# A two-layer decoder kernel: longer ring of PSUM banks, moved copies and scatters, and a causal mask split between TensorE and GpSimd

## What is computed

```python
x = layernorm(x + attention16(layernorm_affine(x)))        # phase 0 (A), 16 heads of 64, 512 x 512 scores
x = layernorm(x + cross16(x, ctx))                         # phase 1 (B), 16 heads, 77 keys
x = layernorm(x + moe_top2(x))                             # phase 2 (C), 8 experts
x = layernorm(x + gated_attention(x))                      # phase 3 (D)
x = layernorm(x + cross8(x, ctx))                          # phase 4 (E), 8 heads, 77 keys
x = layernorm(x + moe_top1(x))                             # phase 5 (F)

def gated_attention(x):                                    # 16 heads of 64
    q, k, v = silu(x @ Wq), silu(x @ Wk), x @ Wv
    cum = cumsum(-softplus(x @ Wa + ba))                   # per head, over the 512 positions
    decay = exp(where(causal, cum[i] - cum[j], -inf))
    o = (q k^T * decay) @ v
    o = groupnorm(o) * gn_w + gn_b                         # per head
    return (o * sigmoid(x @ Wg)) @ Wo
```

## Time and profile before

| | |
|---|---|
| median of 3 runs (lowest, highest) | 1533.67 us (1532.97, 1536.28) |
| the profiled execution's own time | 1532.61 us |
| its span in the trace | 1530.8 us |
| mean granted TensorE clock | 0.927 of full speed |
| PE busy in the span | 83% |
| DVE, ACT, POOL busy in the span | 52%, 55%, 35% |

### The profile page before, as it was taken

The page is one execution under the profiler, slowest core; times in us unless marked ns, Lnnn a source line. Parts: engine busy times, 40 slices in busy tenths (PEclk is TensorE's granted clock), DMA queues, the critical chain, the costliest instruction groups (busy, mean ns, idle before and its releaser), DMA issues. The chain is left out here.

```text
span 1530.8 us, 22554 instructions
## 1 busy us (share of the span) xinstructions
PE 1276.4 (83%) x6934; PEld 735.2 (48%) x6934; DVE 801.0 (52%) x2448; ACT 839.1 (55%) x1902; POOL 530.0 (35%) x606
## 2 busy tenths in 40 slices
PE   5999999999999988877861994899999996786452
PEld 2334443444344335545431993576676764454251
DVE  3543454354334435366653235878675766567425
ACT  4777677767767753554430563567575653453121
POOL 2554455545545531212243351132223222112332
PEclk9999999999999999999885997999999997997686
DMA  8335343330000000000013671100000000000053
GB/s 211 57 62 83 63 71 60 57 80 1 1 1 1 1 1 0 1 1 0 3 58 131 195 208 48 42 1 1 1 1 1 1 1 28 0 1 8 23 153 100
DMA packets 77556, 67.29 MB, mean 44 GB/s; under 512 B 5024, under 2 KB 68640, under 8 KB 77184
## 3 DMA queue, kind: packets, MB, share of 16 engines
q1 hardware_dynamic: 73488, 57.69, 16.6%
q0 software_dynamic: 3520, 7.27, 1.3%
q10 hardware_dynamic: 432, 0.89, 0.2%
HBM read 37.42 MB, written 28.41 MB: 43 GB/s over the span
## 5 line engine op out<-in xcount | busy, mean ns | idle before, releaser
L1960 POOL TENSOR_TENSOR work<-work 128x512 f32<-128x512 f32 x256 | 266.1, 1039 | 271.6 <-DVE work L1438 271.6
L1013 ACT ACTIVATE work<-bank,work 128x512 f32<-128x512 f32 x256 | 176.5, 689 | 116.7 <-DVE work L1430 116.7
L1430 DVE TENSOR_REDUCE work<-bank 128x1 f32<-128x512 f32 x256 | 176.6, 690 | 77.5 <-PE bank L547 77.5
L555 PEld LDWEIGHTS bank<-cst,work 128*128 128x128 f32 x1024 | 110.4, 141 | 163.8 <-issue 103.5
L555 PE MATMUL bank<-cst,work 128*128 128x128 f32 x1024 | 159.7, 283 | 6.3 <-ACT work L1021 6.1
L1438 DVE RECIPROCAL work<-work 128x1 f32<-128x1 f32 x256 | 41.9, 164 | 223.4 <-ACT work L1013 223.1
L1021 ACT ACTIVATE work<-bank 128x512 f32<-128x512 f32 x256 | 152.6, 596 | 0.5 <-PE bank L555 0.5
L547 PE MATMUL bank<-work 64*128 64x512 f32 x512 | 144.5, 641 | 3.4 <-ACT work L1013 3.4
L2000 POOL TENSOR_TENSOR work<-work 128x1232 f32<-128x1232 f32 (+1 forms) x32 | 55.5, 1734 | 254.9 <-DVE work L1512 254.8
L565 PE MATMUL bank<-work 128*64 128x512 f32 x512 | 137.4, 617 | 0.7 <-ACT work L1021 0.7
L494 PE MATMUL bank<-OT,W 128*128 128x512 f32 x208 | 95.7, 604 | 1.2 <-DVE am L1618 0.7
(11 more groups left out here) (258 smaller groups left out, 2443.6 us busy)
## 6 DMA issues: line engine op xcount, KB each, us to landing
xs<-gat SPq DMA_DIRECT2D x18, 1040.0 KB, 13.1
W<-in_w SPq DMA_DIRECT2D x30, 322.0 KB
W<-in_w SPq DMA_DIRECT2D x23, 193.0 KB
work<-xs SPq DMA_DIRECT2D x62, 65.0 KB
gat<-yt SPq DMA_DIRECT2D x12, 256.0 KB, 3.4
work<-in_w SPq DMA_DIRECT2D x9, 322.0 KB
W<-in_v SPq DMA_DIRECT2D x1, 2048.0 KB, 12.3
x_ext<-in_x SPq DMA_DIRECT2D x4, 256.0 KB, 7.5
```

The costliest lines, as they stand in the source:

```text
L555: m = nc.tensor.transpose(out[:, k * P:(k + 1) * P], pA[u % 5][:, k * P:(k + 1) * P], ident)
L1013: A(pA[u % 5], bank[u % 3][:, :], ACT.Exp, bias=nmax[:, u % 8:u % 8 + 1], accum_out=rsum[0][:, u % 8:u % 8 + 1]).then_inc(sem("a_e"), 1)
L1430: V.tensor_reduce(nmax[:, u % 8:u % 8 + 1], bank[u % 3][:, :], AX, ALU.max, negate=True)\
L1960: G.tensor_tensor(pA[u % 5], pA[u % 5], rsum[1][:, u % 8:u % 8 + 1].to_broadcast([P, S]), ALU.mult)\
```

## The change

1. The ring of `take_next` is a list that PE sets anew: banks 5, 6, 7 in phase B, banks 2, 5, 6, 7 in phase E, 5, 6, 7 for the tiles of both moe phases, and 6, 7 again in phase D (and A).
2. On ACT, in a step with t = 1 of a cross phase, the copies of the outputs come ahead of the step's exp.
3. POOL scatters batch 0 at the start of the moe phase, after its part of the last tail, and no longer at u = 15 of the cross loop.
4. In phase D the mask matmul (L821, two a group) is gone. Partitions 96 to 127 of the stationary and the moving operand of L819, unused before, now carry a coarse mask: it puts 1e30 where the row index lies beyond the diagonal's group of 4. POOL fills the groups' masks once at the start of D.
5. What is left above the diagonal, inside each group of 4, POOL zeroes after ACT's exp, with one `affine_select` of 128x512 f32 in place per head (`mask_fine`, two a group); DVE's `d_at` waits for it.
6. `d_decays` is one matmul with a 128-wide stationary operand in place of two with 64. The operands of L811 and L819 were broadcast columns; now POOL writes them out with three copies of 96x128 bf16 a group (`pick`), two groups ahead.
7. DVE's wait for POOL's preparation (`d_zero`) moves from the start of D to just before `d_lsel`; PE waits for `d_zero`, or for the product `d_qe` of two groups before, ahead of `d_decays`. The mask and identity tiles that DVE built at the start of the program are gone.

```diff
         turn = [0]
+        ring = [6, 7]
         def take_next(pe, key, reader, value):
-            i = 6 + turn[0] % 2
+            i = ring[turn[0] % len(ring)]
...
+                ring[:] = [5, 6, 7] if ph == 1 else [2, 5, 6, 7]
                 cross_q(c, 0)
                 cross_kv(c)
...
+                ring[:] = [5, 6, 7]
                 loaded(pe, "w" + m_["n"], DMA_COUNT["w" + m_["n"]])
...
             def d_decays(g):
-                for hh in range(2):
-                    m = mm(out[hh * DH:(hh + 1) * DH, :], sel[:, 2 * p + hh:2 * p + hh + 1].to_broadcast([P, DH]),
-                           lsel_b[b % 2], start=True, stop=True)
-                m.then_inc(sem("d_lp"), 1)
+                if g < 2:
+                    pe.wait_ge(sem("d_zero"), 1)
+                else:
+                    pe.wait_ge(sem("d_qe"), g - 1)
+                out = take(pe, 0, sem("d_el"), g + 1)
+                mm(out[:, :], selE[g % 2][:, :], lsel_b[b % 2], start=True, stop=True).then_inc(sem("d_lp"), 1)
             def d_decay_to(g, hh):
-                mm(out[:, :], sel[:, 2 * p + hh:2 * p + hh + 1].to_broadcast([P, P]), lsel_b[b % 2],
-                   start=True, stop=False)
-                mm(out[:, :], ident_b[:, :], mask[:, :], start=False, stop=True).then_inc(sem("d_la"), 1)
+                mm(out[:, :], selM[2 * (g % 2) + hh][:, :], lsel_b[g // 8 % 2], start=True, stop=True).then_inc(sem("d_la"), 1)
...
+                    if t == 1 and b >= 1:
+                        cross_o(c, b - 1)
                     if b < NB:
                         cross_exp(c, b, t)
-                    if t == 1 and b >= 1:
-                        cross_o(c, b - 1)
...
             def d_at(g):
-                    dve.wait_ge(sem("d_dm"), 2 * g + hh + 1)
+                    dve.wait_ge(sem("d_mk"), 2 * g + hh + 1)
...
                     cross_tail(tail, c["w0"], u)
-                    if u == 15:
-                        moe_scatter(MOE[ph + 1], 0)
...
                 tail(m_["w0"] - 1, 0)
+                moe_scatter(m_, 0)
                 moe_scatter(m_, 1)
...
-                G.memset(lselD, 0.0).then_inc(sem("d_zero"), 1)
+                group = lselD.bitcast(BF16)[3 * 32:P, :]
+                link(G.memset(lselD[0:3 * 32, :], 0.0))
+                link(G.memset(group, 1.0))
+                zero = pool.to_reg(0.0)
+                link(G.affine_select(group, group, [[0, 2 * NT], [1, P]], ALU.is_ge, zero, base=0, channel_multiplier=-4))
+                link(G.affine_select(group, group, [[0, 2 * NT], [-1, P]], ALU.is_ge, zero, base=3, channel_multiplier=4))
+                for i in range(2):
+                    link(G.memset(selE[i][3 * 32:P, :], 0.0))
+                for i in range(4):
+                    link(G.memset(selM[i][3 * 32:P, :], 1e30))
+                    link(G.affine_select(selM[i][3 * 32:P, :], selM[i][3 * 32:P, :], [[1, P]], ALU.is_ge, zero, base=-4,
+                                         channel_multiplier=-4))
+                def pick(g):
+                    for hh in range(2):
+                        h = 2 * (g % 8) + hh
+                        G.tensor_copy(selM[2 * (g % 2) + hh][0:3 * 32, :], sel[0:3 * 32, h:h + 1].to_broadcast([3 * 32, P]))
+                    p = 2 * (g % 8)
+                    return G.tensor_copy(selE[g % 2][0:3 * 32, :].rearrange("k (h d) -> k h d", h=2),
+                                  sel[0:3 * 32, p:p + 2].unsqueeze(2).to_broadcast([3 * 32, 2, DH]))
+                def mask_fine(g, hh):
+                    pool.wait_ge(sem("d_dm"), 2 * g + hh + 1)
+                    dm = v3(dmD[g % 2][:, hh * S:(hh + 1) * S], NT)
+                    G.affine_select(dm, dm, [[0, NT], [1, P]], ALU.is_ge, zero, base=0, channel_multiplier=-1)\
+                        .then_inc(sem("d_mk"), 1)
+                pick(0)
+                pick(1).then_inc(sem("d_zero"), 1)
...
+                mask_fine(0, 0)
+                mask_fine(0, 1)
                 for g in range(32 + 5):
                     b, s = g // 8, g % 8
+                    if g + 2 < 32:
+                        pool.wait_ge(sem("d_dm"), 2 * g + 2)
+                        pick(g + 2)
                     if g < 32:
...
                         G.tensor_tensor(qeD[g % 3], qTD[g % 2], elD[g % 3], ALU.mult).then_inc(sem("d_qe"), 1)
+                    if g + 1 < 32:
+                        mask_fine(g + 1, 0)
+                        mask_fine(g + 1, 1)
```

More of the change, by code:

```diff
@@ L109, in decoder @@
         cst = sb("cst", [P, NKEPT])
-        mask = sb("mask", [P, S], BF16)
-        ident_b = sb("ident_b", [P, P], BF16)
+        selM = [sb(f"selM{i}", [P, P], BF16) for i in range(4)]
+        selE = [sb(f"selE{i}", [P, P], BF16) for i in range(2)]
         sel = sb("sel", [P, H], BF16)
@@ L885, in phase_d @@
             def phase_d():
+                ring[:] = [6, 7]
                 loaded(pe, "D", DMA_COUNT["D"])
@@ L1444, in _ @@
             V.tensor_scalar(x_ext[:, :, D + 1], const("slot")[:, 0:NB * NT], 2.0, None, ALU.mult)
-            V.tensor_copy(ident_b[:, :], ident)
-            V.tensor_copy(sel[:, :], const("sel"))
-            for t in range(NT):
-                i = V.tensor_scalar(mask[:, t * P:(t + 1) * P], after, 1e30, None, ALU.mult)
-            i.then_inc(consts_ready, 1)
+            V.tensor_copy(sel[:, :], const("sel")).then_inc(consts_ready, 1)
             NU = NB * UNITS
@@ L1876, in phase_d @@
                 enter(dve, 3)
-                dve.wait_ge(sem("d_zero"), 1)
                 loaded(dve, "D", DMA_COUNT["D"])
@@ L1884, in phase_d @@
                 d_split_w(2)
+                dve.wait_ge(sem("d_zero"), 1)
                 d_lsel(0)
```

1 line of the change is left out of this document (removed).

## The result

The changed kernel takes 1515.53 us (median of 4 runs, 1513.62 to 1517.65) against 1533.89 us (4 runs): a ratio of 0.9878, 95% interval 0.986 to 0.9896. It is faster by 18.4 us where 50 were forecast. The profiled execution has a span of 1514.4 us, against 1530.8 before.

A forecast was written before the change was run, and what follows sets the result against it. The prediction took D to be bound by PE and B and E to be held by waits for banks, copies and POOL's scatters. It summed 28 (B) + 14 (E) + 8 (D) = 50 us, forecasting 1484, range 1461 to 1516.

The forecast's parts named there:

- PE leaves after the fifth copy, about 5.0 instead of 7.6: Outputs in B: with three banks PE finishes a batch at ACT's copying pace, 2.6 us sooner.
- opening 5: Opening of B: the first 24 us of q, k and v products get 5 us shorter in all.
- the loop's q: q products in B's loop: three times 1.7 us, 5 us, limited by when ACT finishes.
- E's 8: Outputs in E: four pairs written without waiting; three batches give 1.6 + 3.4 + 3.5 = 8 us.
- counted 28: Phase B: terms sum to 33 us, 28 counted because PE then meets DVE's subtraction sooner.
- counted 14: Phase E: terms sum to 21.5 us, only 14 counted because engines wait for each other in turn.
- counted 8: Phase D: half of PE's 17.7 us saving, 9, less 1 for the first uncovered select.
- I keep half, 9: Phase D: of PE's 17.7 us saving 9 stays, since DVE must follow and POOL's added reads hold it.
- (a): Rival: GpSimd's reads hold DVE in D, so the 9 us become -12, giving 1504; chance 0.22.
- (b): Rival: waits removed in B and E return elsewhere, only half kept, 21 + 8 = 29, giving 1504; chance 0.13.
- (c): Rival: all is kept, 33 + 21.5 + 17.7 = 72 us, giving 1461; chance 0.10.
- (d): Rival: slower, a dear select (4.5 us) makes POOL set D's pace, giving 1567; chance 0.05.

The follow-up runs named there:

- part_D: The kernel before with only the change of phase D (the changed kernel with parts 1 to 3 undone): 1537.19 us, ratio 1.0022.
- part_D_late: The kernel before with only the change of phase D, POOL's three copies placed behind the selects: 1528.98 us, ratio 0.9974.
- parts123: The kernel before with the ring, the order of output copies and the scatter changed, phase D untouched: 1513.52 us, ratio 0.9863.
- late_gate_last: The changed kernel with POOL's copies behind the selects and, on PE, k's transposes and the output products ahead of the gate projection: 1515.02 us, ratio 0.9887.
- late_two_copies: The changed kernel with copies behind the selects, two a group, and the two 64-row decay matmuls with broadcast columns back: 1506.13 us, ratio 0.9823.

## Why the prediction was wrong, point by point

**Where the number failed.** Two steps failed, the larger one outside D. "PE leaves after the fifth copy, about 5.0 instead of 7.6" took ACT's copies for the pace and gave PE no price of its own. Eight products of 512 f32 columns take PE 7.03 us without any bank to wait for. This price stood in the kernel before, in L494's row. So q's eight went from 7.70 to 7.13, v's stayed, eight pairs of outputs stop at 7.09, and four pairs in E at 3.65 where 2.6 was forecast. The terms "opening 5", "2.6" and "4" of the outputs, the loop's q and E's 8 lose most of what they held. What stayed is what had been a wait: the exp ahead of the copies (13.7 to 7.1, forecast 5.4, measured 6.6) and part of the end of B.

The same sum has no term for PE's clock in B. The batch at 729, given 4 us, went from 10.29 to 9.42 at a granted 0.75; the last one, given 2.6, went from 7.60 to 8.70 at 0.81. Both follow a wait of over 4 us for ACT, which the change leaves in place.

**B** counted 28. The twelve profiles with the three parts reach the first scores of D at 939.6 to 947.8 us, on average 943.6; the three without any of them (before, part_D, part_D_late) at 954.8 to 958.4, on average 956.5. That is 13. **E** counted 14: its stretch behind D's last scores is 8.7 and 8.5 us shorter in the two profiles of the changed kernel. **All outside D** counted 42, measured 20.3 and, in the second set, 21.0.

**End of B.** The wait for L1618 is gone and L1997 no longer stands behind the scatters, both as said. The outputs begin at 769.20. That is 780.28 - 769.20 = 11.1 us earlier, where 5 + 12 + 5 + 8.8 = 30.8 were to have come forward by then. The cover named for the scatter, POOL's 14.79 us of idle, held: the eight scatters end at 776.04 and the next start at 781.90.

**D** counted 8: measured 1.0 and 0.8 in the two profiles, nothing in the two comparisons by medians (parts123 is as fast), and 3.4 us lost alone, though not in D's length. The saving on PE was about rightly priced: 17.7 forecast, PE busy some 19 to 20.8 us less, and 13.1 us of time when POOL adds nothing. The step that failed is "I keep half, 9", with "behind a waiting POOL stand only pick, d_qe and the group norm's chains, which have about a step". The copies stand ahead of qe and the selects, and where POOL comes late from the chain there is no step to spare. With the copies behind them D is 301.1 and 302.9 us, 8.1 and 6.3 under before. So my 8 is about the value of the change with another order of its own instructions, as long as the three parts outside D are there; alone it is worth 5.8 us of D and 3.5 of the time. The 5.0 us between 301.1 and 296.1 are about what POOL's added work costs D even in the better order.

**The rivals.** (a) named the mechanism, "the second select, the copies and d_qe now stand back to back", and its sign in D against my 8, but with 21 us of damage (9 to -12) where all that POOL gained cost 12.1 (D 296.1 to 308.2), 7.1 of it by order alone; its total of 1504 missed too, as it kept my 42. The Trainium skill (SBUF — State Buffer, Who interferes with whom), cited there, fits the rows: L1823 (two SBUF inputs) is held until the product ends, L1809 (one in PSUM) stays at 0.683. (b), half kept outside D, had the number of its half: 21 forecast, 20.3 measured; with D at 0 it would have given 1513. Its reason holds only in part, so the number was partly luck: in B PE's waits for ACT's L1124 did grow, from 7.8 to 12.7 us, but those for DVE's subtraction did not (9.7 before, 8.9 after), and PE's own price is no wait at all. (c) and (d) are out: no select was near 3.3 us.

**Signs.** Three came as forecast: L710 does not wait for the rank, L1997 is free of the scatters, and the pair L816 and L821 starts 0.22 us apart (947.26 and 947.48). These did not: outputs near 5 and 2.6 us; tiles of C 28 us earlier (8 us, at 835.15); a group near 9.5 us (308.2 / 31 = 9.9); a select near 1.0 us (0.63).

**Open:** why part_D loses 3.4 us with D as long as before, what sets the granted clock in B and C from one execution or set of runs to the next, and whether late_gate_last fails for the reason that I read from its waits.

## What to carry to other kernels

Before a wait is priced by its reader's pace, price the writer alone: find a row where the same instruction runs with nothing to wait for. Work that another engine needs goes ahead of work that is needed two steps later, on an engine with time to spare too. When a change gains nothing, move its own instructions in their queue before giving it up. Tell a phase by its own length, and repeat a profile before a few us are explained: one stretch of lower clock made D 1.8 us longer here, and the match of late_two_copies with its sum rested on it.

## What the runs showed that I had not expected

- An `affine_select` of 128x512 f32 on GpSimd takes 0.63 us, half of the product of two full inputs of that shape (1.28).
- A short wait can be paid for twice on PE. Here 2.16 us of idle was followed by 3.7 us at a granted clock of 0.54, in a phase that runs at 0.98; with a wait of 1.44 us in the same place the clock stayed at 1.00. The wait cost 0.7 us more, the clock 1.6.
- The same program reached one point of its code at 947.8 us in one execution and 942.0 in another, with 0.88 and 0.94 of the clock granted in one 50 us stretch and 0.87 and 0.90 in the tiles of C, while its phase D took 308.2 and 308.4.
